# Cross-attention loop of a decoder layer: scores moved behind the q/k product on TensorE, and the copies out of PSUM moved ahead of reciprocal and row maxima on VectorE

## The reference

```python
x = x + attn(layernorm(x), ...)          # linear attention, gated, relu
# cross-attention, for each sequence
q = hidden @ Wq ; k = ctx @ Wk ; v = ctx @ Wv        # 1024 columns, 16 heads of 64
scores = einsum('bhsd,bhkd->bhsk', q, k) / sqrt(64)
probs = softmax(scores, axis=-1)
out = einsum('bhsk,bhkd->bhsd', probs, v)
x = x + out @ Wo + bo
x = x + ffn(layernorm(x), ...)           # shared swiglu + routed expert (top 1 of 8)
```

## Time and profile before

| | |
|---|---|
| time, median of 3 runs | 692.32 us (692.11 to 692.47) |
| the profiled execution, its own time | 695.6 us |
| its span, first to last instruction | 693.9 us |
| mean granted TensorE clock | 0.972 |
| TensorE busy | 626.8 us (90%), weight loads 504.2 |
| VectorE busy | 416.5 us (60%) |
| ScalarE busy | 418.1 us (60%) |
| GpSimd busy | 308.1 us (44%) |
| instructions | 14738 |

### The profile page before, as it was taken

How to read it: one execution, slowest core, us unless ns; L and a number is a source line. 1 busy time by engine, 2 the same in 40 slices (tenths; PEclk the granted TensorE clock), 3 DMA queues, 4 the chain that set the end, 5 groups by cost and what they waited for, 6 DMA issues and landing times.

```text
span 693.9 us, 14738 instructions
## 1 busy us (share of the span) xinstructions
PE 626.8 (90%) x5159; PEld 504.2 (73%) x5159; DVE 416.5 (60%) x1168; ACT 418.1 (60%) x1499; POOL 308.1 (44%) x331
## 2 busy tenths in 40 slices
PE   3578999999999999999999999999999897978993
PEld 2467888878887788778877887788778675544552
DVE  2768555866676567656765676567545453744442
ACT  2348778666757675767576857685766672423441
POOL 3434543355355435453545354526423533253443
PEclk9889999999999999999999999999999997999997
DMA  7200100000010001000100000000000025134330
GB/s 164 84 19 1 27 2 2 20 9 1 2 52 8 1 2 57 2 1 2 59 1 1 1 33 1 1 1 32 2 1 1 33 90 170 54 103 123 93 89 8
DMA packets 24951, 23.47 MB, mean 34 GB/s; under 512 B 7007, under 2 KB 22497, under 8 KB 24880
## 3 DMA queue, kind: packets, MB, share of 16 engines
q1 hardware_dynamic: 21520, 15.96, 8.4%
q0 software_dynamic: 2784, 6.32, 2.5%
q10 hardware_dynamic: 576, 0.26, 0.5%
HBM read 15.03 MB, written 7.95 MB: 33 GB/s over the span
## 4 chain that ended last, share of the span: by engine, by line
PE 58%; DVE 11%; issue 10%; POOL 9%; ACT 8%; DMA 2%; SPq 1%; another core or an unknown queue 1%; DVEq 0%; POOLq 0%
PE bank L1202 7%; PE bank L1170 7%; PE bank L1191 5%; PE bank L1180 5%; PE bank L1207 5%; PE bank L1288 5%; ACT prob L980 4%; PE bank L1208 4%; PE bank L1209 4%; PE bank L1130 4%; POOL routed L523 3%; PE bank L1073 3%; POOL prob L531 3%; DVE mneg L773 2%; PE bank L1304 2%
## 5 line engine op out<-in xcount | busy, mean ns | idle before, releaser
L980 ACT ACTIVATE prob<-bank,mneg 128x128 f32<-128x128 f32 x512 | 182.6, 381 | 99.6 <-DVE mneg L773 99.5
L531 POOL TENSOR_TENSOR prob<-prob,rden 128x512 f32<-128x512 f32 x128 | 130.7, 1042 | 179.5 <-DVE rden L780 179.4
L980 ACT ACTIVATION_READ_ACCUMULATOR prob<-bank,mneg 128x1 f32 x512 | 112.2, 219 | 0.0
L986 ACT COPY probT<-bank 128x512 f32<-128x512 f32 x128 | 77.0, 601 | 46.5 <-PE bank L1180 45.7
L773 DVE TENSOR_REDUCE mneg<-bank 128x4 f32<-128x512 f32 x128 | 81.4, 678 | 29.1 <-PE bank L1170 29.1
L1170 PE MATMUL bank<-kT,qT 64*128 64x128 f32 x1024 | 74.4, 284 | 6.3 <-ACT prob L980 2.9
L1180 PE MATMUL bank<-ident,prob 128*128 128x128 f32 x512 | 78.1, 275 | 0.1
L1170 PEld LDWEIGHTS bank<-kT,qT 64*128 64x128 f32 x1024 | 62.3, 187 | 18.7 <-issue 12.7
L1191 PE MATMUL bank<-probT,V 128*64 128x128 f32 x1024 | 71.1, 282 | 2.3 <-issue 2.3
L1180 PEld LDWEIGHTS bank<-ident,prob 128*128 128x128 f32 x512 | 60.2, 142 | 15.5 <-issue 14.5
L472 POOL TENSOR_TENSOR rstd<-var_eps,neg_half 128x4 f32<-128x4 f32 x24 | 24.4, 1018 | 96.6 <-DVE var_eps L624 96.6
(11 more groups left out here) (176 smaller groups left out, 1321.4 us busy)
## 6 DMA issues: line engine op xcount, KB each, us to landing
prob<-routed SPq DMA_DIRECT2D x39, 128.5 KB
xin<-in_x_dram SPq DMA_DIRECT2D x8, 256.0 KB, 3.4
ctx_nat<-in_ctx_dram SPq DMA_DIRECT2D x8, 192.0 KB, 4.0
routed<-blank SPq DMA_DIRECT2D x9, 128.5 KB
qT<-in_L_ffn_rt_gate_dram SPq DMA_DIRECT2D x1, 1024.0 KB
qT<-in_L_ffn_rt_up_dram SPq DMA_DIRECT2D x1, 1024.0 KB
out_dram<-probT,prob POOLq DMA_INDIRECT x39
prob<-in_L_xattn_Wq_dram SPq DMA_DIRECT2D x1, 512.0 KB, 8.0
```

The costliest lines, as they stand in the source:

```text
L531: nc.gpsimd.tensor_tensor(view, view, spread(rden[:, m % 2, c * NC:(c + 1) * NC], 2, S), ALU.mult)\
L980: last = nc.scalar.activation(prob[:, m % 2, p * S:(p + 1) * S], bank[c % 2][:, i * S:(i + 1) * S], ACT.Exp, bias=mneg[:, m % 2, p:p + 1], ...
L986: nc.scalar.copy(probT[:, m % 2, c * 512:(c + 1) * 512], made(r1, ("T", m, c))[:])\
```

## The change

On TensorE, in the beats 0 and 2, the scores of the next batch stand behind `make_qk` instead of ahead of it, so directly in front of `prob_v`. On VectorE, `empty_v` and `empty_qk` stand at the head of the beat, ahead of `reciprocal` and the two `row_max`. The other engines' programs are untouched.

```diff
@@ VectorE
             for n in range(FIRST, LAST + 1):
                 for b in range(NC):
+
+                    if b % 2 and live(n + 1):
+                        empty_v(n + 1, b // 2)
+                    if qk_of(n, b) and qk_engine(n, b) == "dve":
+                        empty_qk(*qk_of(n, b))
                     if b == 0 and live(n):
                         reciprocal(n, 1)
                     if b == 2 and live(n + 1):
@@
                     if b % 2 == 0 and live(n + 1):
                         row_max(n + 1, b)
                         row_max(n + 1, b + 1)
-                    if b % 2 and live(n + 1):
-                        empty_v(n + 1, b // 2)
-                    if qk_of(n, b) and qk_engine(n, b) == "dve":
-                        empty_qk(*qk_of(n, b))
                     if b == 1 and live(n - 1):
                         residual(n - 1)
@@ TensorE
                     if live(n):
                         turn_probs(n, b)
-                    if b % 2 == 0 and live(n + 1):
-                        scores(n + 1, b // 2)
                     if b % 2 and live(n + 1):
                         make_v(n + 1, b // 2)
                     if qk_of(n, b):
                         make_qk(*qk_of(n, b))
+
+                    if b % 2 == 0 and live(n + 1):
+                        scores(n + 1, b // 2)
                     if b == 0 and live(n - 1):
                         prob_v(n - 1, 1)
```

## The result

The changed kernel takes 705.06 us (median of 4 runs, 703.92 to 706.83) against 692.3 us of the kernel before (692.11 to 692.47): ratio 1.0187, 95% interval 1.0163 to 1.021. It is slower, by 12.8 us of the medians.

The account below looks back on a forecast made before the run. TensorE, 98% busy, bounds the attention loop unless another engine's chain ends last. Six groups of 1.74 us give 10.4, plus 0.8 and 0.4 is 11.6: median 692.3 becomes 703.9 us, range 694.5 to 708.5.

Parts of the forecast that it names:

- the ends: Outside the six four-batch groups: +0.8 us at the first scores, +0.4 at n = 29; everything behind the loop moves along.
- Saving on TensorE: Scored beats: scores directly before P V, behind the q or k product, save 0.17 us per beat.
- Step 1: Batches n = 14 and 15, four scored beats: VectorE waits for TensorE, so the savings stay, -0.68 us.
- Step 2: n = 16, beat 0: output product could come 0.85 us earlier, but oT allows only 0.2; shift -0.2.
- Step 3: n = 16, beat 2: the copy delays the reciprocal, GpSimd's normalisation, rstd and h; shift +0.42 us.
- Step 4: n = 17, beat 0: copy adds 0.62 us before maxima, exponentials and oT; output product shifts +1.04.
- Step 5: n = 17, beat 2: later scores delay x1's low part and the gate product by +0.7 us; shift +1.74.
- The start: First scores, n = -1, behind a k product: about 0.9 + 0.2 us later, less 0.3 saved up to n = 2: +0.8.
- Rival A: Faster: TensorE bounds everywhere, all 60 beats keep 0.17 us; 682, or 679 with freed waits; chance 0.08.
- B: No change: the saved 0.17 us of all beats and the lost waits cancel; 691 to 694 us; chance 0.05.
- C: Milder: delays of steps 3 and 4 overlap, +2.4 to +4.8 us; with the start 695 to 698; chance 0.15.
- D: Heavier: TensorE's order saves nothing, oT is 0.62 us late, 2.4 per group; 708 us; chance 0.15.

Follow-up runs that it names:

- scores in the middle of Q: Against the kernel before, TensorE makes the scores between the two halves of the q or k product, VectorE as before; 696.05 us, one run.
- three beats back: Against the changed kernel, VectorE's q or k copy stands behind the maxima in three of eight scored beats per four batches; 693.67 us, 0.9975 of before.
- reciprocal put first: Against the changed kernel, VectorE's reciprocal stands ahead of the copy again, the maxima stay behind it; 702.95 us, 1.0103 of before.
- copy back in one beat: Against the changed kernel, VectorE's copy stands behind the maxima only in n = 1 modulo 4, beat 0; 702.22 us, one run.

## Why the prediction was right

Forecast 703.9, measured 705.06, with the five steps within 0.05 us each in the group that was walked through. The loop came out as forecast (11.5 against 11.6), but the ends did not: the profiled execution, forecast at 707.2, took 704.38, since TensorE had more of its clock behind the loop. That the median came out so close is in part luck, and so are two sums below.

- **Saving on TensorE**, 0.17 per scored beat: 0.19 (2.52 to 2.33). Shown, and that it goes with the number of changes of shape, by the scores in the middle of Q.
- **Step 1**, -0.68 and the fifth beat: -0.83 at P of n = 16. Shown by the rows. Two errors cancel here: the five beats give 0.99 together (0.20 in each of the first four), and two odd beats of n = 14, behind the last product of q, became 0.08 longer each, which the prediction doesn't have and no experiment explains.
- **Step 2**, the saving is given back for oT: -0.18 at the output product, wait 0.47. Shown by the rows, and the three beats back take it away.
- **Step 3**, +0.42 through GpSimd: +0.45. Shown by the reciprocal put first. The steps are the same, and GpSimd's rows came 5.69 and 5.65 later (341.55 and 348.64 against 335.86 and 342.99), less the 5.21 of the groups ahead +0.48 and +0.44.
- **Step 4**, +0.62 for oT: +0.60. Shown by the copy back in one beat (0.57).
- **Step 5**, +0.70: +0.73. Shown by its being undone (0.74 of the period, although not by the time).
- **The start**, +0.8: mis-sized. The mark at n = 5 is 0.96 later, where 0.8 and the 1.04 of step 4 would have made 1.84; so the start gave about -0.1. The first exponentials come at 50.34 instead of 49.69, 0.65 later and not 1.1, and the output product of n = 1 starts at 80.25, where 80.40 stood before. Why so little is lost there is not shown. The last stretch, n = 25 to 29, took 1.66 more (64.19 against 62.53), where 0.7 for step 5 and 0.42 for h make 1.1. At its end, from h to the mark of n = 29, TensorE took 5.03 us (556.24 to 561.27) against 4.63 before (545.18 to 549.81): 0.40 more, with a granted clock of 0.50 from 557 to 559 us, where before it was 1.00. The prediction has no term for the clock. The errors of the ends nearly cancel, and that is luck.
- **The medians** are 12.8 apart, the profiles 8.8, the loop 11.5. The 1.3 that the medians have over the loop I can't place; it is within what the profiles vary from n = 29 to the end (141.4 to 144.9). That the profiles are only 8.8 apart is the granted clock behind the loop, 0.95 after against 0.92 before.

Rival A fell at the place that was named: the output product had 0.15 of room. B fell with the period, which is 1.77 longer and not the same. C fell, since the delays of steps 3 and 4 do add. D fell, since the order saves what it was taken to save.

## What to carry to other kernels

An engine that is 60% busy isn't free at every place: look for the instructions that have no idle time ahead of them, for only there does a reordering on it move the start of what follows, and it moved by 0.60 us for a copy of 0.69. A wait for a bank that TensorE shows (here 0.50 for the k copy) is worth nothing if the next instruction waits for something else that the cure makes later. And two halves of one change must be measured apart: TensorE's half was harmless, VectorE's alone cost four times the whole, and of what it cost in the change, three of eight beats carried all.

## What the runs showed of the hardware that I had not expected

Passing once less between whole-array, 64-row and 64-column products is worth 0.19 us (T to P 2.33 us against 2.52, and 2.53 in an order that restores the number of changes).

TensorE's granted clock falls behind waits inside the loop, in some kernels and not in others. In VectorE's order alone it was 0.50, the lower of its levels of 1.2 and 2.4 GHz, from 384 to 387 us, right behind the wait of 2.27, and the two gate products at 384.06 took 2.08 us instead of 1.12. It fell again, to 0.79 from 555 to 570 us, behind 28 us in which TensorE had been busy for 82% of the time. In the profile of the change it was 0.50 from 557 to 559 us, behind waits of 1.73 (552.29) and 1.76 (556.24). In TensorE's order alone a wait as long, 1.74 at 539.64 us, had no fall behind it: the granted clock stayed 1.00 until 576 us. From 128 to 500 us, where TensorE was busy for 97% of the time before and 93% after the change, it was 1.00 in both. Where it falls, a wait costs more than its own length; in the change this was 0.40 of 11.5 us. These are observations of single profiles; no experiment was made on the clock.
